# Mamba, expert, window-attention and gated-FFN layers in one kernel: routing moved to the head, part of sequence 1's scans moved among the experts' tiles, units reordered inside every turn and at the end

## The reference, cut to what matters

```
xn = layernorm(x)
x  = x + mamba(xn) + experts(xn)        # layer 0
xn = layernorm(x)
x  = x + window_attention(xn) + gated_ffn(xn)   # layer 1

mamba:   proj = xn @ in_proj.T ; hs, gate = split(proj)            # 256 + 256
         u = silu(conv4(hs) + b) ; x_dbl = u @ x_proj.T            # dt | B | C = 64 | 16 | 16
         dt = softplus(rmsnorm(dt) @ dt_proj.T + b) ; B, C = rmsnorm(B), rmsnorm(C)
         for n in 0..15:  h_n[t] = exp(dt[t] * A_n) * h_n[t-1] + dt[t] * u[t] * B[t,n]
         y = sum_n h_n * C_n + u * D ; out = (y * silu(gate)) @ out_proj.T
experts: e = argmax(xn @ gate_w.T + b) ; out = relu(xn @ w1[e] + b1[e]) @ w2[e] + b2[e]   # one of 8 experts per token
window_attention: 16 heads of 8, keys within 32 positions of the query, softmax, @ Wo
gated_ffn: (silu(xn @ Wg.T) * (xn @ Wu.T)) @ Wd.T, hidden 384
```

## Time and profile before

| | |
|---|---|
| median of 3 runs | 1000.43 us (1000.12 to 1002.18) |
| the profiled execution: its time / its span | 1001.08 us / 999.3 us, mean granted TensorE clock 0.928 |
| busy share of the span | PE 80%, DVE 76%, ACT 64%, POOL 44% |
| head, to the first scan step | 78.8 us |
| turn 0 from there, to step 0 of sequence 1 | 166.2 us |
| turn 1, to step 0 of sequence 2 | 110.4 us |
| turns 2 to 6, to step 0 of sequence 7 | 480.7 us, 95.0 to 97.7 each |
| turn 7 to its step 15, and the rest | 75.5 us and 87.7 us |

### The profile page before, as it was taken

How to read it: one execution, slowest core, us unless ns; L and a number is a source line. 1 busy time by engine, 2 the same in 40 slices (tenths; PEclk the granted TensorE clock), 3 DMA queues, 4 the chain that set the end, 5 groups by cost and what they waited for, 6 DMA issues and landing times.

```text
span 999.3 us, 15614 instructions
## 1 busy us (share of the span) xinstructions
PE 797.0 (80%) x5226; PEld 548.1 (55%) x5226; DVE 758.9 (76%) x1059; ACT 638.5 (64%) x1976; POOL 437.8 (44%) x248
## 2 busy tenths in 40 slices
PE   0955689677489798979898989898988996798775
PEld 0732678676165366546555655565556554555543
DVE  7569445543577988899888888998898788887485
ACT  0224356644269767966796689578947893795563
POOL 2257432110556337624851584258425852672100
PEclk9957799998699989999999999999999997999897
DMA  6535699875244244424433442345245414640000
GB/s 209 189 119 189 206 265 310 244 213 153 65 123 97 85 100 134 104 80 121 130 93 97 127 124 70 106 129 131 52 124 142 104 47 121 157 112 23 18 11 12
DMA packets 85952, 123.20 MB, mean 123 GB/s; under 512 B 8560, under 2 KB 43760, under 8 KB 85744
## 3 DMA queue, kind: packets, MB, share of 16 engines
q1 hardware_dynamic: 79584, 115.38, 41.5%
q0 software_dynamic: 6288, 6.82, 3.0%
HBM read 106.21 MB, written 12.29 MB: 119 GB/s over the span
## 4 chain that ended last, share of the span: by engine, by line
PE 36%; DVE 20%; POOL 15%; issue 13%; ACT 9%; DMA 3%; SPq 3%; DVEq 0%; POOLq 0%; ACTq 0%
POOL hc L1221 8%; DVE hst L823 7%; PE y_bank L1319 4%; PE more L1451 4%; PE work L1338 4%; DVE dBu L815 3%; POOL xs_d L1189 3%; ACT pexp L1123 3%; POOL x_res L1205 2%; SPq L604 2%; ACT dA L1045 2%; PE work L1364 1%; PE work L1297 1%; PE work_l L1290 1%; PE work L1463 1%
## 5 line engine op out<-in xcount | busy, mean ns | idle before, releaser
L1221 POOL TENSOR_TENSOR hc<-hst,bcr 128x1024 f32<-128x1024 f32 x116 | 276.9, 2387 | 397.6 <-DVE dBu L815 375.3
L823 DVE TENSOR_TENSOR_SCAN hst<-dA,dBu 128x1024 f32<-128x1024 f32 x128 | 291.7, 2279 | 0.9 <-ACT dA L1045 0.3
L1045 ACT ACTIVATE dA<-dt,neg_a 128x511 f32<-128x511 f32 x256 | 170.7, 724 | 13.3 <-DVE hst L823 10.7
L815 DVE TENSOR_TENSOR dBu<-dtu,bcr 128x1024 f32<-128x1024 f32 x128 | 161.8, 1264 | 19.6 <-DMA bcr<-bc_d 9.7
L1319 PE MATMUL y_bank<-pk,hc 128*128 128x128 f32 x1024 | 144.2, 287 | 27.1 <-POOL hc L1221 26.3
L1319 PEld LDWEIGHTS y_bank<-pk,hc 128*128 128x128 f32 x1024 | 122.2, 148 | 64.8 <-POOL hc L1221 39.4
L1451 PE MATMUL more<-pk,pexp 128*96 128x128 f32 x480 | 103.5, 290 | 26.2 <-ACT pexp L1123 20.7
L1451 PEld LDWEIGHTS more<-pk,pexp 128*96 128x96 f32 x480 | 56.5, 125 | 66.1 <-issue 29.2
L1136 ACT COPY pT<-more 96x512 f32<-96x512 f32 x120 | 69.9, 583 | 34.5 <-PE more L1451 34.2
L1123 ACT ACTIVATE pexp<-work_l,nmax 128x96 f32<-128x96 f32 x240 | 78.5, 345 | 9.5 <-DVE nmax L970 9.4
L1123 ACT ACTIVATE pexp<-work,nmax 128x96 f32<-128x96 f32 x240 | 77.7, 335 | 2.6 <-DVE nmax L970 2.6
(11 more groups left out here) (363 smaller groups left out, 1517.2 us busy)
## 6 DMA issues: line engine op xcount, KB each, us to landing
bcr<-bc_d SPq DMA_DIRECT2D x128, 512.0 KB, 5.1
qbd<-in_wx SPq DMA_DIRECT2D x8, 578.0 KB, 4.6
o_all<-in_wx SPq DMA_DIRECT2D x8, 578.0 KB, 5.3
pT<-in_wx SPq DMA_DIRECT2D x8, 578.0 KB, 4.7
kT<-in_wx SPq DMA_DIRECT2D x8, 578.0 KB, 4.5
vw<-in_wx SPq DMA_DIRECT2D x8, 578.0 KB, 5.1
xs_d<-rbuf POOLq DMA_DIRECT2D x1, 2560.0 KB, 9.7
hst<-in_hidden SPq DMA_DIRECT2D x8, 256.0 KB, 5.3
```

The source lines that it names most:

```text
L815: v.tensor_tensor(dBu[:], dtu[par], bcr[n % RING][:, 0:1, :].to_broadcast([P, NH, L]), ALU.mult).then_inc(s_dBu, 1)
L823: v.tensor_tensor_scan(hst[n % 2][:].rearrange("p h t -> p (h t)"), dA[n % 2][:].rearrange("p h t -> p (h t)"), dBu[:].rearrange("p h t -> ...
L1045: s.activation(dA[n % 2][:, h, 1:L], dt[par][:, h, 1:L], ACT.Exp, scale=neg_a[:, h, n:n + 1]).then_inc(s_dA, 1)
L1221: g_.tensor_tensor(hc[n % 2][:], hst[n % 2][:], bcr[n % RING][:, 1:2, :].to_broadcast([P, NH, L]), ALU.mult).then_inc(s_hc, 1)
```

## The change

What the diff does, part by part:

1. **Head.** All of the norms, gate logits, `pick`, `count`, `place` and the first 8 scatters now stand in `LEAD`, ahead of turn -1. SP loads the four hidden blocks before the packed weights, and the constants come after the norms. The other 24 scatters go to slots 9 and 10 of turn -1. The table is zeroed from dA[1], and the scatters wait for that, not `pick`.
2. **Turn 0** is four slots longer; tiles start at slot 2 and are spread over slots 2 to 31. `AHEAD`: slot 26 holds `y_end` and `gated` of sequence 0 and `init` of sequence 1, slots 27 to 31 hold scan steps 0 to 4 of sequence 1. Turn 1 leaves out what was done ahead.
3. **Every turn.** `xdr` behind step 8 of slot 10, `bc` in slot 10; the row maximum of slot 8 ahead of `ss`; in slots 7, 8 and 10 the y sums behind `turn`; step 15's product with C on GpSimd, behind the scan; `up2` in bank 5, the bank of `fin` and `pre`.
4. **End.** `fg` to `fh` and `rden` of sequence 6 leave turn 7 and stand between the links of sequence 7's chain. In the 16 groups the FFN of sequence 7 goes to 2 to 7 with buffers of its own, `avg` to 7, `fin` and `ffn_down` are spread one piece per group, and the last groups have an order of their own with one more bank (`oM`).

```diff
-MOE_AT = 4
+MOE_AT = 2
...
-MID = {2: [("scan", "slots", 0)], 8: [("pre", "ss", 0)], 18: [("pre", "dw", 0)], 20: [("pre", "dt", 0)], 23: [("pre", "dtu", 0)]}
+MID = {2: [("scan", "slots", 0)], 8: [("pre", "ss", 0)], 10: [("pre", "xdr", 0)], 18: [("pre", "dw", 0)], 20: [("pre", "dt", 0)], 23: [("pre", "dtu", 0)]}
...
-        9: [("pre", "xdr", 0), ("pre", "bc", 0), ("scan", "rows", 1)],
-        10: [("pre", "zg0", 0)], 11: [("pre", "sg0", 0), ("scan", "rows", 2)],
+        9: [("scan", "rows", 1)],
+        10: [("pre", "bc", 0), ("pre", "zg0", 0)], 11: [("pre", "sg0", 0), ("scan", "rows", 2)],
...
-ROWMAX_MID = (20,)
+ROWMAX_MID = (8, 20)
+SUM_LAST = (7, 8, 10)
...
-LAST_AT = {0: [("v2", 0), ("v3", 0)], 3: [("avg", 0)], 4: [*[("fin", j) for j in range(NT)], ("y_out", 0)], 6: [("fg", 0), ("fs", 0), ("fu", 0), ("fh", 0)], 8: [("fg", 1), ("fs", 1), ("fu", 1), ("fh", 1)], 10: [("fg", 2), ("fs", 2), ("fu", 2), ("fh", 2)],
-           12: [("ffn_down", 0)], 13: [("proj", 0), ("proj", 1)],
-           16: [("proj", 2), ("y_last", 2), ("values", G - 3), ("own", G - 4), ("own", G - 3)],
-           18: [("values", G - 1), ("own", G - 2), ("own", G - 1), ("proj", 3), ("y_last", 3)]}
+LAST_AT = {0: [("v2", 0), ("v3", 0)],
+           2: [("fg", 0), ("fu", 0)], 3: [("fs", 0), ("fh", 0)], 4: [("fg", 1), ("fu", 1)], 5: [("fs", 1), ("fh", 1)],
+           6: [("fg", 2), ("fu", 2)], 7: [("fs", 2), ("fh", 2), ("avg", 0)],
+           8: [("fin", 0)], 9: [("fin", 1)], 10: [("fin", 2)], 11: [("fin", 3), ("y_out", 0)],
+           12: [("ffn_down", 0)], 13: [("ffn_down", 1), ("proj", 0)], 14: [("ffn_down", 2), ("proj", 1)], 15: [("ffn_down", 3)]}
+FFN_UNITS = ("fg", "fs", "fu", "fh", "rden")
...
-        units += [("scan", "sum", m) for m in range(N - 1) if SUM_AT[m] == slot]
+        sums = [("scan", "sum", m) for m in range(N - 1) if SUM_AT[m] == slot]
+        units += sums if slot not in SUM_LAST else []
...
         units += [(lane, "turn", g) for lane, g in of("exp", slot)]
+        units += sums if slot in SUM_LAST else []
...
-    out = [("y_end", 0, a), ("rdT", 0, f), ("gated", 0, a), ("yT", 0, a)]
-    out += [(name, 0, a) for name in ("out", "x1", "ln_a", "ln_b", "q", "k", "v0", "v1")]
-    for t in range(G + 3):
-        if 1 <= t <= G:
+    out = [("y_end", 0, a), ("fg", 0, f), ("fu", 0, f), ("gated", 0, a), ("fs", 0, f), ("fh", 0, f), ("yT", 0, a),
+           ("fg", 1, f), ("out", 0, a), ("fu", 1, f), ("x1", 0, a), ("ln_a", 0, a), ("fs", 1, f), ("fh", 1, f),
+           ("fg", 2, f), ("fu", 2, f), ("ln_b", 0, a), ("fs", 2, f), ("fh", 2, f), ("rden", 0, f), ("rdT", 0, f)]
+    out += [(name, 0, a) for name in ("q", "k", "v0", "v1")]
+    for t in range(G):
+        if t >= 1:
             out.append(("exp", t - 1, a))
-        if t < G:
-            out.append(("scores", t, a))
-        if 2 <= t < G + 2:
+        out.append(("scores", t, a))
+        if t >= 2:
             out += [("scale", t - 2, a), ("turn", t - 2, a)]
-        if O_LAST <= t < G:
+        if t >= O_LAST:
             out.append(("own", t - O_LAST, a))
-        if t < G:
-            out.append(("rowmax", t, a))
-        out += [(name, k, f if name in ("avg", "attnT", "fin", "y_out") else a) for name, k in LAST_AT.get(t, [])]
+        out.append(("rowmax", t, a))
+        out += [(name, k, f if name in ("avg", "fin", "y_out") else a) for name, k in LAST_AT.get(t, [])]
+    out += [(name, k, a) for name, k in (
+        ("exp", G - 1), ("scale", G - 2), ("turn", G - 2), ("values", G - 3), ("proj", 2), ("own", G - 4),
+        ("scale", G - 1), ("turn", G - 1), ("own", G - 3), ("values", G - 2), ("y_last", 2), ("own", G - 2),
+        ("values", G - 1), ("own", G - 1), ("proj", 3), ("y_last", 3))]
...
-LEAD = [("stats", 0), ("stats", 1), ("norm", 0), ("stats", 2), ("norm", 1)]
+ROUTE_CONSTS = 12
...
+def lead():
+
+    out = [("stats", 0)]
+    for k in range(B):
+        if k + 1 < B:
+            out.append(("stats", k + 1))
+        out += [("norm", k), ("xT", k)]
+        if k > 0:
+            out.append(("gate", k - 1))
+    out += [("gate", B - 1), ("route_consts", 0), ("consts", 0), ("pick", 0), ("count", 0), ("place", 0)]
+    return out + [("scatter", k) for k in range(2)]
...
+AHEAD = 5
+SLOTS_0 = SLOTS + AHEAD - 1
+
+
+def ahead():
+
+    at = {SLOTS - 2: [("y_end", 0, 0), ("gated", 0, 0), ("init", 0, 1)]}
+    for n in range(AHEAD):
+        at[SLOTS - 1 + n] = [("step", n, 1), ("product", n, 1)]
+        if n >= 2:
+            at[SLOTS - 1 + n].append(("sum", n - 2, 1))
+        at[SLOTS - 1 + n].append(("spread", n, 1))
+    return at
+
+
+AHEAD_AT = ahead()
+DONE_AHEAD = {unit[:2] for units in AHEAD_AT.values() for unit in units}
+
+
+LEAD = lead()
...
-    for k in range(B):
-        if k + 3 < B:
-            put(-1, k, ("stats", k + 3))
-        if k + 2 < B:
-            put(-1, k, ("norm", k + 2))
-        put(-1, k, ("xT", k))
-        if k > 0:
-            put(-1, k, ("gate", k - 1))
-    put(-1, B, ("gate", B - 1))
-    put(-1, B + 1, ("pick", 0))
-    put(-1, B + 2, ("count", 0))
-    put(-1, B + 3, ("place", 0))
-    put(-1, 14, ("scatter", 0))
+    put(-1, 9, ("scatter", 2))
+    put(-1, 10, *[("scatter", k) for k in range(3, B)])
     put(0, MOE_AT, ("gather", 0), ("xt", 0))
     for m in range(NM + 2):
-        slot = MOE_AT + m * (SLOTS - MOE_AT) // (NM + 2)
+        slot = MOE_AT + m * (SLOTS_0 - MOE_AT) // (NM + 2)
...
-           "oL": 0, "gate0": 1, "up0": 2, "gate1": 0, "up1": 1, "gate2": 2, "up2": 0}
+           "oL": 0, "gate0": 1, "up0": 2, "gate1": 0, "up1": 1, "gate2": 2, "up2": 5}
...
+FFN_BANK = {"gate0": 5, "up0": 6, "gate1": 7, "up1": 5, "gate2": 6, "up2": 7}
...
             if key == "xnT":
-                done1(eng, b + LAG["pre"] - 1 - LAG["finish"], "fin")
+                done1(eng, b + LAG["pre"] - 1 - LAG["attn"], f"up{HC - 1}")
...
-            for slot in range(SLOTS if it < B else 0):
-                for lane, name, k in PLAN_AT[slot]:
+            for slot in range(0 if it >= B else SLOTS_0 if it == 0 else SLOTS):
+                for lane, name, k in PLAN_AT[slot] if slot < SLOTS else []:
+                    if it == 1 and (name, k) in DONE_AHEAD:
+                        continue
                     b = it - LAG[lane]
                     if name in ("slots", "rows") and b == 0:
                         b = B
+                    if it == B - 1 and lane == "attn" and name in FFN_UNITS:
+                        continue
                     if not isinstance(b, int) or 0 <= b < B:
                         yield name, k, b, LAG[lane] % 2
+                if it == 0:
+                    for name, k, b in AHEAD_AT.get(slot, []):
+                        yield name, k, b, b % 2
...
-            x_load(0)
-            x_load(1)
+            for k in range(4):
+                x_load(k)
             sp.dma_start(pk[:], pack).then_inc(s_pack, 16)
-            x_load(2)
-            x_load(3)
-            sp.dma_start(ffn_i, ffn_d).then_inc(s_ffn, 16)
 
             def weights(m):
                 e = sp.value_load(tile_e[0:1, m:m + 1], min_val=0, max_val=E - 1)
             def early(name, k):
                 if name == "norm":
                     sp.wait_ge(s_axn, (k + 1) * NT)
-                    sp.dma_start(seq(xn_d, k), xna[k]).then_inc(s_xast[k], 16)
                     if k + 4 < B:
                         x_load(k + 4)
-                    if k == 0:
+                    sp.dma_start(seq(xn_d, k), xna[k]).then_inc(s_xast[k], 16)
+                    if k == 4:
+                        sp.dma_start(ffn_i, ffn_d).then_inc(s_ffn, 16)
                         sp.wait_ge(s_xast[0], 16)
                         sp.dma_start(x_in[:], seq(xn_d, 0)).then_inc(s_xin, 16)
-                elif name == "scatter":
+                elif name == "scatter" and k == 0:
                     sp.wait_ge(s_route, ROUTE_TILES)
                     for m in range(3):
                         weights(m)
...
                                      dBu[:].rearrange("p h t -> p (h t)"), 0.0,
                                      ALU.mult, ALU.add).then_inc(s_h, 1)
-                if n == N - 1:
-                    dve.wait_ge(s_h, b * N + N)
-                    dve.wait_ge(s_hc, b * N + N - 1)
-                    dve.wait_ge(s_ys, b * (N + 1) + N - 1)
-                    v.tensor_tensor(hc[n % 2][:], hst[n % 2][:], bcr[n % RING][:, 1:2, :].to_broadcast([P, NH, L]),
-                                    ALU.mult).then_inc(s_hc, 1)
...
 
             def pre(name, b, par):
                 if name == "xnT":
+                    if b == 0:
+                        act.wait_ge(s_const, ROUTE_CONSTS)
                     full0(act, b, name)
                     s.copy(xnT[:, 1:1 + L], bank0[:]).then_inc(s_free0, 1)
...
             def zero_slots():
-                pool.wait_ge(s_constp, 1)
+                pool.wait_ge(s_const, 8)
```

(27 more changed lines are left out.)

127 lines of the change are left out of this document (77 added, 50 removed).

## The result

The changed kernel takes 991.97 us (median of 4 runs, 988.8 to 994.0) where the kernel before, on the same chip, takes 1001.3: a ratio of 0.9892, 95% interval 0.987 to 0.9915. It is faster by 9 us, where I had forecast 35. The time lies outside the range.

The account below looks back on a forecast made before the run. No engine bounds alone: waits hopping between PE, VectorE and ScalarE do, plus turn 0's joint stalls and the lone last chain. To sequence 2 -6.7, turns 2 to 6 -13, end -15.5: -35.2 from 1001.1, or 966 us; range 948 to 984.

Parts of the forecast that it names:

- Each normal turn, slots 7 to 12: Middle of a turn: step 8 no longer waits for the powers; 0.7 us of PE's product waits won per turn.
- The turn's end: Product 15 to next step 0: product goes to GpSimd, up2 stops waiting for fs; 8.8 to 6.9, -1.9 us.
- The order at the port: Behind scan 15: dtu goes before GpSimd's product, which ends 3.5 us behind the scan; otherwise the turn ends 2.3 later.
- the slower rival: In the turns: dBu meets GpSimd's products, 1.9 us each; three per turn cost 40, five give 1033 us; chance 0.07.
- The distance from the last scatter to the first add: Head: 10.7 us as in the kernel before, so last scatter at 94 puts the first add at 105.
- about nothing, because the earlier start pays them: Turn 0: price of moving five scan steps among the tiles; last add at 244, before 242.9.
- fin and ffn_down: Last turn's 16 groups: spreading them in pieces over groups with some slack wins 1.8 and 1.7 us.
- the three waits for the tanh go: Last turn's 16 groups: these waits in the feed-forward vanish, -2.2 us.
- Behind the last row maximum: End of kernel: last groups' values and own interleaved, so 12.7 us become about 8, -4.8 us.
- should hold the full clock: Last turn, x1 to first row maximum: PE with FFN matmuls in its gaps keeps full clock, -1.4 us (0 to -3).
- The turns give back more: Rival: if rowmax, scores and sums in slots 7 to 12 move up, each turn wins 5; 950 us, chance 0.17.
- Wrong would be: Signs: tiles over 2.9 us without a step, dBu of 2 to 3, powers-to-product wait holding PE longer than before.

Follow-up runs that it names:

- sum_slot11: The changed kernel with the sum over step 7's product moved from slot 10 to slot 11, behind that slot's scores on TensorE; 978.47 us, 0.9737.
- product_dve: The changed kernel with the last product of a turn back on VectorE, but behind dtu; 1002.76 us, 0.998.
- up2_bank0: The changed kernel with a normal turn's up2 matmul back in bank 0 and xnT waiting for fin again; 991.12 us, 0.9882.
- ahead1: The changed kernel with one scan step of sequence 1 put into turn 0 instead of five; 986.91 us, 0.9828.
- last_fin_whole: combined_up2 with all of fin in group 8 and all of ffn_down in group 12 of the last turn; 972.61 us, 0.9699.
- combined_up2: The changed kernel with step 7's sum in slot 11, last-turn FFN chunks whole, one step ahead, up2 in bank 0; 967.56 us, 0.9658.

## Why the prediction was wrong, point by point

For turns 2 to 6 the forecast was -13 us and the profiles show -2.4. By places:

| turns 2 to 6, sum of five | forecast | measured |
|---|---|---|
| step 15 to 0 | -9.5 | -10.8 |
| steps 7 to 11 | -3.5 | +4.9 |
| step 0 to 1 | 0 | +6.9 |
| steps 3 to 5 | 0 | -3.4 |

- **Each normal turn, slots 7 to 12: the step that failed.** I knew that "PE's sum there still needs the product that GpSimd makes behind the powers", and took the wait as staying as it was, with 0.7 us won. Making the scan earlier does not make that product earlier: GpSimd's powers begin 3.7 us behind step 7 where they had begun 3.5 behind it, and product 7 ends at 9.3 instead of 9.0. The sum now stands ahead of work that VectorE needs at once; steps 7 to 10 took 20.8 us on average instead of 19.8. Shown by sum_slot11: with the sum behind the next scores they take 19.0.
- **The clock was put at nothing, and that is the larger part.** Where the clock stays up in the middle the edits still won 0.4 us (5.2 + 8.4 + 5.8). What made them lose was the low clock behind TensorE's wait, some 6 to 7 us over the five turns (an estimate: 138.8 us for steps 7 to 11 against five times the 26.4 to 26.6 of a turn without it). Another 6.9 us lie in step 0 to 1 of turns 3, 5 and 6. My sum had no term for either, though the earlier trace rows showed a granted clock of 0.96; the five turns went from 0.97 to 0.95, and to 1.00 in sum_slot11.
- **Luck.** The 3.4 us in steps 3 to 5 were forecast by nobody and hid a part of the loss.
- **A reading.** "No engine has a tenth to spare by itself" misreads: TensorE's 85 of 96.6 us are 88%, VectorE's 83 are 86%, ScalarE's 72 are 75%. The sum does not rest on it.
- **The turn's end** was right in mechanism and size: -1.9 forecast, -2.05 measured; by product_dve 1.1 of it is the product, and up2_bank0 puts up2's bank at 0.6 to 0.8 in four of five turns. The order at the port was right too: the product took 3.25 us, dtu 1.20. The Trainium skill (SBUF — State Buffer, Who interferes with whom) has a two-input VectorE instruction and a GpSimd one that reads SBUF exclude each other. The trace agrees: the product began 0.17 us into dtu's 1.20 and took 3.25, where it takes 2.35 alone, so it ran once dtu was over. The collisions of the slower rival came once a turn (dBu 2.42 at 394.28), not three times, and sum_slot11, with two a turn (2.43 and 2.12), is faster. That the low clock falls on the turn's start is shown to depend on up2's bank; why it comes in some turns and not in others stays open.
- **Head and turn 0.** The distance from the last scatter to the first add was mis-sized: 10.7 carried over, 17.1 measured (109.27 - 92.13). The 139 us of tiles, 17 behind the last add and 19 to step 5 held within 1.2 us. But that the steps ahead cost "about nothing, because the earlier start pays them" hid a loss: ahead1 shows them to cost more than they save.
- **The 16 groups.** fin and ffn_down were nearly right (-3.5 forecast; last_fin_whole is 2.7 to 3.1 us longer). That "the three waits for the tanh go" for -2.2 was wrong: each wait went, but both halves of a chunk stayed in the loop, in a group each, 2.9 us with the low clock.
- **Behind the last row maximum** -4.8 was -3.6; x1 and the stretch to the first row maximum did not come earlier, as matmuls of sequence 6's FFN (1.60 and 1.02 us at 913.17 and 914.61) stand ahead of yT, and the clock is 0.87 to x1 and 0.77 behind it. That PE "should hold the full clock" there did not come true: it was 0.77 before as well, and up2_bank0, with the same matmuls but 1.00 to x1, takes 11.3 us to x1 instead of 12.7.
- **The rivals.** None had this. "The turns give back more" named the product wait as its obstacle; the obstacle did not stay the same, it grew, as the last sign under "Wrong would be" has it.

In combined_up2 the stages of the table stand at -5.7, -18.1, -3.7, +2.1, -2.0, -2.2 and -3.2, -32.8 us in all: near the sum that I had made, by a kernel that differs in four places, and with 3.4 us in its turns from steps 3 to 5.

## What to carry to other kernels

When an early step is pulled further forward, look at the in-order queue of the engine that consumes the late producer's result, and put that consumption behind all that others wait for. Price a new wait of TensorE twice: its length, and the matmuls behind it at half the clock. Compare two runs stage by stage before a difference is given to an edit: here up to 5 us came and went at a place that no edit touched. A piece of work cut in two in a loop that runs through two engines lengthens two rounds; keep it whole unless one half lies outside the loop.

## What the hardware showed beyond that

- The low clock also came behind gaps well under the 3.7 us of the kernel before: 2.09 us in the middle of a turn, 2.33 us among shorter ones at its end, and 0.77 us with one of 0.28 ahead of steps 3 to 5. The same gaps in the same slots were followed by it in some sequences and not in others. Taken away at a turn's start it came more often elsewhere (up2_bank0), without a gain in time.
- The low clock's length differed: in windows of 0.5 us it lasted some 3.5 us behind one long gap (446.2 to 449.6 before) and behind the 2.09 us in the middle (395.5 to 398.9 after), and some 7 us behind the spread gaps of a turn's end (446.7 to 453.5 after), although TensorE was busy for most of all three.
- GpSimd's powers (rr, 128 x 12) took 2.27 and 2.31 us in the head, before and after, with VectorE idle, and 3.18 to 3.44 in every turn of both kernels, where each time they began while a dBu of VectorE was running (389.91 to 391.14 in the turn shown above, the powers from 390.09) or 0.01 us ahead of it. That fits the exclusion between product and dtu.
